# Residual additions by accumulating DMA transfers from GpSimd, and a maximum over contiguous elements

## What is computed

```
y = affine(conv1x1(x, fc1_w, fc1_b), fc1_s, fc1_t)
nodes = windows of 8 x 8 of y                      # (Bw, 64, C)
idx = top_k(-dist(normalised nodes), 9)
feat = concat([x_i, x_j - x_i])
h = max over neighbours of gelu(affine(feat @ ew.T + eb, es, et))
x1 = affine(conv1x1(h, fc2_w, fc2_b), fc2_s, fc2_t) + x
h = relu(bn(w1 @ x1)); h = relu(bn(depthwise3x3(h, wd))); out = x1 + bn(w2 @ h)
```

## Time and profile before

| | |
|---|---|
| median of 3 runs | 4837.28 us (4835.97 to 4840.45) |
| the profiled execution | 4838.94 us, its span 4837.1 us |
| TensorE busy | 4619.9 us, 96% |
| VectorE busy | 4693.2 us, 97% |
| ScalarE busy | 3791.8 us, 78% |
| GpSimd busy | 486.5 us, 10% |
| mean granted TensorE clock | 0.99 of full speed |
| 16 DMA engines, mean busy share of a queue | 5.7% (83.58 MB in all, 17 GB/s) |
| chain that ended last | PE 55%, DVE 20%, issue 13%, ACT 10% |

### The profile page before, as it was taken

The page is one execution under the profiler, slowest core; times in us unless marked ns, Lnnn a source line. Parts: engine busy times, 40 slices in busy tenths (PEclk is TensorE's granted clock), DMA queues, the critical chain, the costliest instruction groups (busy, mean ns, idle before and its releaser), DMA issues.

```text
span 4837.1 us, 87468 instructions
## 1 busy us (share of the span) xinstructions
PE 4619.9 (96%) x28416; PEld 2567.8 (53%) x28416; DVE 4693.2 (97%) x5293; ACT 3791.8 (78%) x7749; POOL 486.5 (10%) x260
## 2 busy tenths in 40 slices
PE   5999999999999999999999999999999999999996
PEld 3555555555555555555555555555555555555543
DVE  3799999999999999999999999999999999999998
ACT  4878877887877878878878878878878788788773
POOL 0101101001011010111001010110100101110200
PEclk9999999999999999999999999999999999999997
DMA  1000000000000000010000000000000000100000
GB/s 44 14 16 19 11 26 11 19 19 18 17 14 24 11 21 17 11 28 11 18 21 12 23 13 18 19 18 19 13 24 11 21 17 11 28 11 11 14 6 12
DMA packets 33519, 83.58 MB, mean 17 GB/s; under 512 B 4674, under 2 KB 4930, under 8 KB 29956
## 3 DMA queue, kind: packets, MB, share of 16 engines
q1 hardware_dynamic: 33028, 77.38, 5.7%
HBM read 52.20 MB, written 25.17 MB: 16 GB/s over the span
## 4 chain that ended last, share of the span: by engine, by line
PE 55%; DVE 20%; issue 13%; ACT 10%; DVEq 0%; SPq 0%; DMA 0%; ACTq 0%; POOL 0%; POOLq 0%
DVE acc L930 13%; PE pg L537 11%; PE pmisc L458 8%; DVE hid L916 6%; PE pg L540 6%; PE pmisc L442 5%; PE pvu L524 4%; PE pself L549 3%; PE pmisc L466 2%; PE pmisc L461 2%; ACT diag L753 2%; PE pself L552 2%; ACT MV L706 2%; PE pmisc L403 2%; ACT g L722 2%
## 5 line engine op out<-in xcount | busy, mean ns | idle before, releaser
L930 DVE SCALAR_TENSOR_TENSOR acc<-hpad,w,acc 128x1024 f32<-128x1024 f32 (+1 forms) x2560 | 2917.3, 1174 | 25.8 <-ACT acc L738 25.8
L916 DVE TENSOR_REDUCE hid<-g 128x192 f32<-128x1728 f32 x512 | 1609.4, 3143 | 0.5 <-ACT g L728 0.5
L537 PE MATMUL pg<-MV,VU 128*128 128x512 f32 x2048 | 1149.5, 643 | 41.1 <-ACT VU L713 37.4
L722 ACT ACTIVATE g<-pg 128x512 f32<-128x512 f32 x1536 | 911.8, 594 | 239.4 <-DVE hid L916 150.9
L706 ACT ACTIVATE MV<-pone,cst 64x512 f32<-64x512 f32 x1024 | 694.6, 678 | 9.6 <-PE pone L510 0.4
L442 PE MATMUL pmisc<-x,w 96*128 96x384 f32 (+1 forms) x1536 | 649.3, 505 | 10.3 <-ACT hpad L653 5.7
L540 PE MATMUL pg<-MV,VU 128*64 128x512 f32 x2048 | 531.4, 595 | 36.2 <-ACT g L722 36.0
L653 ACT ACTIVATE hpad<-pmisc,sh,sc 128x384 f32<-128x384 f32 (+1 forms) x768 | 505.2, 658 | 47.2 <-PE pmisc L442 21.0
L458 PE MATMUL pmisc<-acc,w 128*96 128x256 f32 x2048 | 512.8, 394 | 25.2 <-ACT acc L745 22.8
L442 PEld LDWEIGHTS pmisc<-x,w 96*128 96x128 f32 x1536 | 268.9, 192 | 421.5 <-issue 297.2
L458 PEld LDWEIGHTS pmisc<-acc,w 128*96 128x96 f32 x2048 | 319.1, 165 | 290.4 <-issue 140.8
(11 more groups left out here) (97 smaller groups left out, 5142.7 us busy)
## 6 DMA issues: line engine op xcount, KB each, us to landing
xin<-in_x_dram SPq DMA_DIRECT2D x32, 768.0 KB, 5.7
xres<-in_x_dram SPq DMA_DIRECT2D x128, 192.0 KB, 2.5
out_dram<-res SPq DMA_DIRECT2D x128, 192.0 KB, 2.1
g<-in_consts_dram SPq DMA_DIRECT2D x1, 640.0 KB
w<-in_p_dram SPq DMA_DIRECT2D x1, 570.5 KB
w<-in_p_dram SPq DMA_DIRECT2D x1, 259.2 KB
g<-in_rows_dram SPq DMA_DIRECT2D x1, 218.2 KB
cst<-in_consts_dram SPq DMA_DIRECT2D x1, 72.5 KB
```

The lines of the kernel that those rows point to most:

```text
L537: last = nc.tensor.matmul(ps[:, :], VU[:, r, part, 0:ONE128], cols[part], start=True, stop=True)
L722: nc.scalar.activation(g[:, p % 2, part, 0:KN, :], pg[(3 * p + part) % 2][:, :].rearrange("p (k n) -> p k n", k=KN), ACT.Gelu).then_inc(ge ...
L916: nc.vector.tensor_reduce(hid[:, c % 2, j, :, :], g[:, r].rearrange("p c k n -> p c n k"), op=ALU.max, axis=AX.X).then_inc(hid_ready, 1)
L930: nc.vector.scalar_tensor_tensor(out=dst, in0=src, scalar=wk, in1=dst, op0=ALU.mult, op1=ALU.add).then_inc(tap_done, 1)
```

## The change

1. The fc2 job has no identity product. ScalarE evacuates fc2's result with its bias to `x1`; then GpSimd, in the same pair, waits for that evacuation and issues a DMA transfer that adds the chunk of x from DRAM to `x1` in place (`accum_op=ALU.add`, `add_input`). `xres` and SP's 128 loads of it are gone. The first w1 job of a strip waits for the completion of these transfers (`x1_sum`) for chunks 2t + 1 and 2t + 2.
2. The w2 job has no identity product. After two w2 jobs GpSimd issues a transfer that adds a chunk of `x1` to `res` in place (`add_x1`, offsets 15 and 17); SP waits for it (`out_sum`) and stores one pair later than before (offsets 16 and 18). The program is one pair longer at its end.
3. `MV` and `g` are laid out node first, neighbour last. `maxima` reads 9 neighbours in a row for each of 192 outputs. `onehot` reads `pone` with a step of 64 elements between neighbours and writes in order; `gelu` writes runs of 8 elements with one left out between them; `gelu_self` writes single elements with a step of 9. The products read the columns of `MV` in order, as before.

```diff
-STORE_AT = {o + 1: q for o, q in W2_AT.items() if q % 2 == 1}
+ADD_AT = {o + 1: q for o, q in W2_AT.items() if q % 2 == 1}
+STORE_AT = {o + 2: q for o, q in W2_AT.items() if q % 2 == 1}
...
-        xres = sb("xres", [C, 4, CW])
...
-        MV = sb("MV", [128, 2, 2, KN + 1, NODES])
-        g = sb("g", [128, 2, 3, KN + 1, NODES])
+        MV = sb("MV", [128, 2, 2, (KN + 1) * NODES])
+        g = sb("g", [128, 2, 3, NODES, KN + 1])
...
-                    if p % 4 == 2:
-                        bc, c = (b, (p - 6) // 4) if p >= 6 else (b - 1, CHUNKS - 1)
-                        bl, cl = (bc, c + 4) if c < 4 else (bc + 1, c - 4)
-                        if valid(bc, B) and valid(bl, B):
-                            fb, fp = when(b, p, 1)
-                            sp.wait_ge(misc_evac, job_at(fb, fp, "fc2", c))
-                            sp.sem_inc(sp_passed, 1)
-                            load_res(bl, cl)
-
                     for o, t, s, q in due_in(STORE_AT, b, p):
-                        fb, fp = when(b, p, 1)
-                        sp.wait_ge(misc_evac, job_at(fb, fp, "w2", q))
+                        sp.wait_ge(out_sum[q // 2], 16 * (s + 1))
...
+            def add_input(b, p, bc, c):
+
+                pool.wait_ge(misc_evac, job_at(b, p, "fc2", c))
+                pool.sem_inc(pool_passed, 1)
+                nc.gpsimd.dma_start(x1v[:, c * CW:(c + 1) * CW], xv[bc, :, c * CW:(c + 1) * CW],
+                                    accum_op=ALU.add).then_inc(x1_sum[c % 4], 16)
+
+            def add_x1(b, p, o, t, s, q):
+
+                fb, fp = when(b, p, 1)
+                pool.wait_ge(misc_evac, job_at(fb, fp, "w2", q))
+                pool.sem_inc(pool_passed, 1)
+                c = 2 * t + q // 2
+                nc.gpsimd.dma_start(res[:, q // 2, :], x1v[:, c * CW:(c + 1) * CW],
+                                    accum_op=ALU.add).then_inc(out_sum[q // 2], 16)
...
+                    for o, t, s, q in due_in(ADD_AT, b, p):
+                        add_x1(b, p, o, t, s, q)
                     if p % 16 in XN_AT and valid(bi, B):
                         stationary_copy(bi, 4 * h + XN_AT[p % 16])
+                    if p % 4 == 1:
+                        bc, c = (b, (p - 5) // 4) if p >= 5 else (b - 1, CHUNKS - 1)
+                        if valid(bc, B):
+                            add_input(b, p, bc, c)
...
                     if gr == 0 and m == 0:
 
-                        c = min(2 * t + 2, CHUNKS - 1)
-                        fb, fp = when(b, p, w1_slot(0, 0) + (3 if c % 2 == 0 else 7))
-                        pe.wait_ge(misc_evac, job_at(fb, fp, "fc2", c))
+                        for c in range(2 * t + 1 if t else 0, min(2 * t + 2, CHUNKS - 1) + 1):
+                            pe.wait_ge(x1_sum[c % 4], 8 * (s - t) + 16 * (c // 4 + 1))
...
-
-                    row = STRIP * t + 4 * q
-                    last = nc.tensor.matmul(ps[0:C, 0:4 * W], eye128[0:C, 0:C], x1[:, row:row + 4, :],
-                                            start=False, stop=True)
...
-                    last = nc.scalar.activation(MV[h:h + 64, p % 2, w, 0:KN, :], pone[h:h + 64, :, :], ACT.Relu,
+                    last = nc.scalar.activation(MV[h:h + 64, p % 2, w, 0:KN * NODES].rearrange("p (n k) -> p n k", k=KN),
+                                                pone[h:h + 64, :, :].rearrange("p k n -> p n k"), ACT.Relu,
                                                 bias=nbias[h:h + 64, :], scale=1.0)
...
-                nc.scalar.activation(g[:, p % 2, part, 0:KN, :],
-                                     pg[(3 * p + part) % 2][:, :].rearrange("p (k n) -> p k n", k=KN),
+                nc.scalar.activation(g[:, p % 2, part, :, 0:KN],
+                                     pg[(3 * p + part) % 2][:, :].rearrange("p (n k) -> p n k", k=KN),
                                      ACT.Gelu).then_inc(gelu_done, 1)
...
-                nc.scalar.activation(g[:, p % 2, :, KN, :],
+                nc.scalar.activation(g[:, p % 2, :, :, KN],
...
-                nc.vector.tensor_reduce(hid[:, c % 2, j, :, :], g[:, r].rearrange("p c k n -> p c n k"),
-                                        op=ALU.max, axis=AX.X).then_inc(hid_ready, 1)
+                nc.vector.tensor_reduce(hid[:, c % 2, j, :, :], g[:, r], op=ALU.max, axis=AX.X).then_inc(hid_ready, 1)
```

More of the change, by code:

```diff
@@ L225, in build @@
         VU = sb("VU", [128, 2, 2, O])
-        MV = sb("MV", [128, 2, 2, KN + 1, NODES])
-        g = sb("g", [128, 2, 3, KN + 1, NODES])
-        gflat = g[:, 0].rearrange("p c k n -> p (c k n)")
+        MV = sb("MV", [128, 2, 2, (KN + 1) * NODES])
+        g = sb("g", [128, 2, 3, NODES, KN + 1])
+        gflat = g[:, 0].rearrange("p c n k -> p (c n k)")
         c16f = gflat[:, 0:C16]
-        r97 = g[0:C + 1, 1].rearrange("p c k n -> p (c k n)")[:, 0:3 * O]
+        r97 = g[0:C + 1, 1].rearrange("p c n k -> p (c n k)")[:, 0:3 * O]
         hid = sb("hid", [128, 2, PPC, 3, NODES])
@@ L248, in build @@
         xin_load = [sem(f"xin_load{k}") for k in range(2)]
-        xres_load = [sem(f"xres_load{k}") for k in range(4)]
+        x1_sum = [sem(f"x1_sum{k}") for k in range(4)]
+        out_sum = [sem(f"out_sum{k}") for k in range(2)]
         store_done = [sem(f"store_done{k}") for k in range(2)]
@@ L283, in load_half @@
                 sp.dma_start(xin[:, h, :], xv[b, :, h * 4 * CW:(h + 1) * 4 * CW]).then_inc(xin_load[h], 16)
-            def load_res(b, c):
-                sp.dma_start(xres[:, c % 4, :], xv[b, :, c * CW:(c + 1) * CW]).then_inc(xres_load[c % 4], 16)
             sp.dma_start(w97[:, :], p97).then_inc(w97_load, 16)
@@ L305, in image @@
                         load_half(b + 1, h)
-                    if isinstance(b, int) and b == -1 and p >= 28:
-                        load_res(0, p - 28)
-                    if p % 4 == 2:
-                        bc, c = (b, (p - 6) // 4) if p >= 6 else (b - 1, CHUNKS - 1)
-                        bl, cl = (bc, c + 4) if c < 4 else (bc + 1, c - 4)
-                        if valid(bc, B) and valid(bl, B):
-                            fb, fp = when(b, p, 1)
-                            sp.wait_ge(misc_evac, job_at(fb, fp, "fc2", c))
-                            sp.sem_inc(sp_passed, 1)
-                            load_res(bl, cl)
                     for o, t, s, q in due_in(STORE_AT, b, p):
-                        fb, fp = when(b, p, 1)
-                        sp.wait_ge(misc_evac, job_at(fb, fp, "w2", q))
+                        sp.wait_ge(out_sum[q // 2], 16 * (s + 1))
                         sp.sem_inc(sp_passed, 1)
@@ L335, in _ @@
             pool.wait_ge(consts_ready, 2)
+            xv = x.rearrange("b c row col -> b c (row col)")
+            x1v = x1[:, :, :].rearrange("c row col -> c (row col)")
+            def add_input(b, p, bc, c):
[10 more added lines that the diff above has]
+                                    accum_op=ALU.add).then_inc(out_sum[q // 2], 16)
             def inverse_norms(b, p, bi, h):
@@ L421, in shared_job @@
                                          stop=False)
[L422 to L429, removed]
+                    last = nc.tensor.matmul(ps[0:C, :].rearrange("p (q n) -> p q n", q=PPC), fc2T[:, 0, :],
+                                            hc[:, :, 0:2, :].rearrange("p q win n -> p q (win n)"), start=False,
+                                            stop=True)
                 elif kind == "w1":
@@ L460, in shared_job @@
                     u = 64 * (q // 2)
-                    nc.tensor.matmul(ps[0:C, 0:4 * W], w2T[u:u + 64, FULL, :],
+                    last = nc.tensor.matmul(ps[0:C, 0:4 * W], w2T[u:u + 64, FULL, :],
                                      acc[u:u + 64, par, FULL, (q % 2) * 4 * W:(q % 2 + 1) * 4 * W],
-                                     start=False, stop=False)
-                    row = STRIP * t + 4 * q
-                    last = nc.tensor.matmul(ps[0:C, 0:4 * W], eye128[0:C, 0:C], x1[:, row:row + 4, :],
-                                            start=False, stop=True)
+                                     start=False, stop=True)
                 last.then_inc(misc_ready, 1)
@@ L534, in gather @@
                 r = p % 2
-                cols = [MV[:, r, w, 0:KN, :].rearrange("p k n -> p (k n)") for w in range(2)]
+                cols = [MV[:, r, w, 0:KN * NODES] for w in range(2)]
                 if part < 2:
@@ L548, in gather_self @@
                 for w in range(2):
-                    nc.tensor.matmul(pself[:, 64 * w:64 * w + 64], VU[:, r, w, 0:ONE128], MV[:, r, w, KN, :],
+                    nc.tensor.matmul(pself[:, 64 * w:64 * w + 64], VU[:, r, w, 0:ONE128], MV[:, r, w, KN * NODES:],
                                      start=True, stop=True)
@@ L552, in gather_self @@
                     last = nc.tensor.matmul(pself[64 * w:64 * w + 64, 128:192], VU[:, r, w, ONE128:O],
-                                            MV[:, r, w, KN, :], start=True, stop=True)
```

(8 more changed lines are left out.)

## The result

The change brought 1.5%: 4765.84 us (4760.55 to 4771.52, median of 4 runs) beside 4836.96 us of the kernel before on the same chip, ratio 0.9852 (0.9835 to 0.9869). The forecast was 4590 us, 5.1% less. The direction was right and the time lies in the range, but less than a third of the forecast gain came; the time was off by 176 us. The profiled execution has a span of 4769.8 us.

A forecast was written before the change was run, and what follows sets the result against it. VectorE (4693 us) was taken to set the end, TensorE 5% behind. Afterwards TensorE's 4237 us + 102 at the ends + 160 stalls + 86 remaining waits made 4585, plus 5 at the end: 4590 us, range 4430 to 4810.

The forecast's parts named there:

- The reduction: VectorE's maximum, read in order: 2025 ns instead of 3143, saving 572 us, so VectorE falls to 4121 us.
- onehot: ScalarE's strided PSUM read: taken as no dearer, 678 ns; bounds 0 to 339 us over the run.
- (1): Rival: strided onehot is slow, ScalarE reaches 4195 us and all waits stay; about 4735 us, chance 0.24.
- (2): Rival: the reduction gets no faster, VectorE keeps 4693 us; about 4835 us, chance 0.09.
- gelu_self: ScalarE's single-element writes 36 bytes apart: 0 in the forecast, 64 us more as upper bound.
- L: Time from the fc2 evacuation's end to the transfer's semaphore: taken as 4.5 us, bounds 2.5 to 10.6.
- the stalls: TensorE waiting at first w1 products of strips 0, 1, 2: 10 us per image, 160 in all (72 to 453).
- Rival (3): Slower because L is long: passes 4848 us from L = 9.9 us, 4883 at the bound; chance 0.10.
- 257 us are waits in the middle: TensorE's span less its own 4478 us and 102 at both ends, taken as waits, some 5%.
- a third: Part of TensorE's 257 us of waits kept once VectorE is relieved: 86 us.
- The identity products: Removed from TensorE's fc2 jobs (110 us) and w2 jobs (131 us): 241 us, leaving 4237 us.
- the very end: Additions into res, not waited for by TensorE, cost about 5 us once at the run's end.

The follow-up runs named there:

- dense_self: Changed kernel with jobs sorted fc2 first, w1 last, gelu_self written in order to its own tile, own column left out of the maximum: 4526.31 us, ratio 0.9348.
- busy_wait: Changed kernel plus extra unused matmul products ahead of the three waits for the x1 sums: 4680.95 us, ratio 0.9677.
- max_only: Kernel before with only the node-first layout and contiguous maximum, both residuals still identity products: 4728.23 us, ratio 0.9781.
- late_wait: Changed kernel with the wait for chunk 2t + 2 moved from the first w1 product to the third, one pair later: 4538.39 us, ratio 0.9378.

## Why the prediction was off

- **The reduction** and **onehot**: right. 1946 ns against 2025 forecast, VectorE 4098 us against 4121, onehot 680 ns. Rivals (1) and (2) are out. `gelu_self` stood in a bound only, with 0.65 ns more for each element; it is 1.0 ns, worth 13 to 19 us by dense_self.
- **L and the stalls**: right. L is 4.3 us here, 4.5 forecast; the waits are 135 us in the trace and 143 by the runs, 160 forecast. Rival (3) needed 9.9 us. The transfer lands in 3.6 us, as the forecast's 2.5 + 1.1 had it. But the sentence that the first w1 product reads chunk 2t + 2 (and the same reason in the part on the kernel before) was taken from the program's wait, and is wrong: the third one does. The price stayed as forecast, since the wait stands there; that it could be had for nothing was missed.
- **What the stalls do to the clock**: the step that failed most, a term that was missing. The working added each stall's length and let the work behind it run on at full speed. It ran at 1.2 GHz: 85 us by busy_wait, 100 us by the mean clocks. The kernel before had a granted clock of 1.00 in the middle; only its last 137 us, with TensorE busy for 96 of them, had 0.75. That row gave the hint, and the forecast did not use it.
- **"257 us are waits in the middle", of which "a third" stays**: the second step that failed. max_only, with VectorE at 87% and no stalls, should have had 4478 + 102 + 86 = 4666; it took 4728, so 148 of the 257 us stayed. Less than half of the 257 were waits. The busy time on the profile's page gives TensorE's standing still: 4837 - 4620 - 102 = 115 us in the middle. The windows show the same, 114 us, and 54 for max_only (same columns as above; first the kernel before, then max_only):

```profile
300.00:4700.00 4400.00, 4285.60 (x26587) 2384.47 (x26586) 4380.34 (x4921) 3538.62 (x7237) 463.86 (x234) 1.00 0.06 17
```

```profile
300.00:4583.00 4283.00, 4229.09 (x26490) 2378.33 (x26490) 3806.23 (x4899) 3568.95 (x7209) 268.28 (x232) 1.00 0.06 17
```

Much of the rest is TensorE's own work, mis-sized from one smooth pair. Between 1000 and 4000 us of the kernel before, 491 w1 jobs of one product each have a mean of 0.72 us from start to next start, 0.715 in max_only, and the 0.64 of the earlier trace rows is at their short end. They are 12 of the 14 jobs of a strip, 768 x 0.075 = 58 us; the other two take 0.55 us in max_only, 128 x 0.09 = 11 less. The 0.74 us in late_wait's rows above (2007.99 to 2008.73) is the usual w1 job. The fc1 and inv jobs take 0.04 and 0.07 us more than they were put at, 14 us. So the 148 are 54 of standing still, 47 of w1 jobs, 14 of these, and 33 that are not assigned; by the same prices they lie in the first 300 and the last 140 us.
- **The identity products** at 241 us: 190 when nothing stalls, 112 to 115 of 110 and 68 to 80 of 131. The step counted a product's start-to-start time as gained, and the products behind it took some of it.

In numbers, from the forecast: 4590 + 62 (148 us kept, not 86) + 51 (products 190, not 241) + 85 (clock) - 17 (stalls 143, not 160) = 4771, beside 4766 measured. Each term is a difference of two runs on the way from max_only over late_wait and busy_wait to the changed kernel, so that the sum closes is no proof; the 5 us over are those that the forecast had put at the very end. A split in another order could shift some us between the terms.

So the delivered change is a gain of 106 to 109 us by the maximum, a gain of 190 by two transfers, and a loss of 227 by where one wait stands.

## What to carry to other kernels

A wait of TensorE was paid twice here: with its length, and with half speed behind it; 3 us of standing still was followed by up to 7 us at 1.2 GHz. Before costing a wait, look which product really reads what is waited for, and put it there: that was worth 4.8% here, and a filling with useless products still 1.8%. Size an engine's own work by the mean over all its jobs and not by the smoothest pair, or waits appear that no relief of another engine can take away; and hold the waits so found against the busy time on the profile's page, which here allowed 115 us and not 257.

## What the hardware showed

- An accumulating transfer of 192 KB issued by GpSimd: 0.73 us from the producer's end to the issue, 0.80 us on GpSimd, 3.6 us to landing (3.5 with both operands in SBUF), 2.5 for the plain load, and 4.3 us from the producer's end to the consumer.
- ScalarE reads PSUM with a step of 256 bytes as fast as in order, 680 against 678 ns for 512 elements. The Trainium skill ("PSUM — Partial Sum Buffer", the table of properties) names only matmuls as slowed by patterns that are not contiguous; this read is not.
- ScalarE writes single fp32 elements to SBUF with a step of 36 bytes at 518 ns for 192, against 326 in order: 1.0 ns more for each by their lengths. Runs of 8 cost nothing (596 ns, 594 before).
- VectorE's `feat`, with two small SBUF inputs, takes up to 0.59 instead of 0.16 us beside a GpSimd copy.
